# A graph and feed-forward layer on one core: score buffer moved behind x's parts, and one row tile rounded a step later

## What is computed

```python
xn = layernorm(x)
support = xn @ W                                      # graph layer
g = segment_sum(support[src] * edge_weight[:, None], dst)   # 42500 edges
q = xn @ Wq.T + bq; k = xn @ Wk.T + bk; v = xn @ Wv.T + bv  # 16 heads of 64
q /= norm(q); k /= norm(k)                            # norms of the whole matrices
s = (phi(q) * phi(k)).sum(-1)                         # phi: exp of a map per head
x = x + g + s * v / s
r = act_quant(layernorm(x))                           # rows rounded to 8 bits
x = x + act_quant(silu(r @ Wg.T) * (r @ Wu.T)) @ Wd.T # Wg, Wu, Wd ternary
```

## Time and profile before

| | us |
|---|---|
| median of 3 runs | 1653.69 (1653.36 to 1654.15) |
| the profiled execution, whole | 1655.15 |
| its span, first to last instruction | 1653.4 |
| PE busy in it | 1623.9 |
| DVE busy | 1132.4 |
| ACT busy | 497.1 |
| POOL busy | 713.9 |

### The profile page before, as it was taken

The page is one execution under the profiler, slowest core; times in us unless marked ns, Lnnn a source line. Parts: engine busy times, 40 slices in busy tenths (PEclk is TensorE's granted clock), DMA queues, the critical chain, the costliest instruction groups (busy, mean ns, idle before and its releaser), DMA issues.

```text
span 1653.4 us, 21995 instructions
## 1 busy us (share of the span) xinstructions
PE 1623.9 (98%) x7680; PEld 1336.2 (81%) x7680; DVE 1132.4 (68%) x2622; ACT 497.1 (30%) x640; POOL 713.9 (43%) x577
## 2 busy tenths in 40 slices
PE   7999999899999999999999999999999999999998
PEld 6899999688878888887888888888888888887665
DVE  7887793476787776656555566677757667576796
ACT  4644311222121111114211113333423324233554
POOL 2011555677777777777678605533130120300200
PEclk9999999899999999999999999999999999999999
DMA  9999888765686756557866656577383563742954
GB/s 315 352 410 354 294 269 261 204 139 126 134 210 149 198 131 151 148 142 168 230 148 130 137 154 196 162 189 197 101 195 116 124 161 99 158 127 76 240 157 125
DMA packets 164010, 304.94 MB, mean 184 GB/s; under 512 B 62856, under 2 KB 103624, under 8 KB 163945
## 3 DMA queue, kind: packets, MB, share of 16 engines
q1 hardware_dynamic: 77853, 204.77, 38.9%
q0 software_dynamic: 80272, 82.55, 24.3%
q10 hardware_dynamic: 5820, 16.88, 2.9%
HBM read 202.88 MB, written 101.24 MB: 184 GB/s over the span
## 4 chain that ended last, share of the span: by engine, by line
PE 76%; DMA 12%; DVE 5%; issue 4%; POOL 2%; SPq 1%; ACT 0%; DVEq 0%; POOLq 0%; ACTq 0%
PE PS L402 24%; PE PS L404 24%; PE PS L403 24%; DMA A_dense<-zeros 5%; DMA A_dense<-wtot,cell 5%; POOL A_dense L747 2%; PE PS L1886 2%; PE PS L1916 1%; DVE fin L1572 1%; DMA X<-in_x 1%; DVE stats L1157 1%; DMA rt<-z 1%; DVE hid L1546 0%; DVE ring L1176 0%; DVE h_sc L1549 0%
## 5 line engine op out<-in xcount | busy, mean ns | idle before, releaser
L747 POOL DMA_INDIRECT A_dense<-wtot,cell x333 | 537.6, 1615 | 217.4 <-DMA A_dense<-wtot,cell 123.0
L402 PE MATMUL PS<-AL,SH 125*128 125x500 f32 x784 | 306.3, 391 | 0.0
L404 PE MATMUL PS<-AH,SH 125*128 125x500 f32 x784 | 305.1, 389 | 0.0
L403 PE MATMUL PS<-AH,SL 125*128 125x500 f32 x784 | 304.6, 389 | 0.0
L402 PE MATMUL PS<-WL,xtH 128*125 128x512 f32 x640 | 252.5, 394 | 0.7 <-DVE xtL L1296 0.7
L403 PE MATMUL PS<-WH,xtL 128*125 128x512 f32 x640 | 252.1, 394 | 0.0
L404 PE MATMUL PS<-WH,xtH 128*125 128x512 f32 x640 | 251.9, 394 | 0.0
L1033 ACT ACTIVATE SH<-S 125x1024 fp32r<-125x1024 f32 x98 | 104.0, 1061 | 333.0 <-PE PS L404 333.0
L1410 DVE TENSOR_TENSOR SL<-S,SH 125x1024 fp32r<-125x1024 f32 x98 | 119.6, 1220 | 120.3 <-ACT SH L1033 120.1
L404 PEld LDWEIGHTS PS<-AH,SH 125*128 125x128 f32 x784 | 147.8, 189 | 31.4
L403 PEld LDWEIGHTS PS<-AH,SL 125*128 125x128 f32 x784 | 147.1, 188 | 31.0
(11 more groups left out here) (202 smaller groups left out, 2660.2 us busy)
## 6 DMA issues: line engine op xcount, KB each, us to landing
A_dense<-zeros POOLq DMA_DIRECT2D x40, 1280.0 KB, 9.1
xt<-xnT SPq DMA_DIRECT2D x60, 500.0 KB, 6.2
Araw<-A_dense SPq DMA_DIRECT2D x100, 250.0 KB, 2.7
Aside<-A_dense SPq DMA_DIRECT2D x100, 250.0 KB, 3.0
keyrow<-key_rows SPq DMA_DIRECT2D x42, 512.0 KB, 4.2
ewrow<-weight_rows SPq DMA_DIRECT2D x42, 512.0 KB, 5.5
xnT<-XT ACTq DMA_DIRECT2D x20, 500.0 KB, 8.2
zx<-in_x SPq DMA_DIRECT2D x20, 448.0 KB
```

The costliest lines, as they stand in the source:

```text
L402: nc.tensor.matmul(o, lh, rl, start=start, stop=False)
L403: nc.tensor.matmul(o, ll, rh, start=False, stop=False)
L404: return nc.tensor.matmul(o, lh, rh, start=False, stop=stop)
L747: pool.indirect_dma_start(cells[m], bass.IndirectOffsetOnAxis(cell[:, col:col + 1], 0), wtot[:, col:col + 1], None, compute_op=ALU.add).th ...
```

## The change

The parts of x now start at 196800: `xt` (to 204800), `xtH` and `xtL` of slot 0 (to 212800) and of slot 1 (to 220800). `ex` and `zx` follow (220800 to 228992), so that now the second half of `ex`, the one of odd tiles, lies over `zeros`. `bdk` moves to the last 4096 bytes of `Gs` (214720 to 218816), under the two parts of slot 1. DVE's wait for the strips goes from before the first write of `xtL` of slot 1 to before the first write of the second half of `ex`, at t == 1 and behind its wait for tile 1's products. In the feed-forward part the fourth tile of the last group is rounded at step 14 and not 13; `largest_r` goes from the end of step 12 to the end of step 13, `round_r` and `scales_back` to the end of step 14.

```diff
@@ -78,7 +78,7 @@
-ROUNDED_AT = (8, 10, 12, 13)
+ROUNDED_AT = (8, 10, 12, 14)
@@ -211,16 +211,16 @@
-    bdqk = (bdq, zone("E1f", at, END_AT)("bdk", [P, KT, P]))
     late = E_AT + 20 * D
     assert at <= late
-    ex = zone("E1x", late, END_AT)("ex", [P, 2, D])
-
-    zx = zone("E2x", late, END_AT)("zx", [P, 2, D])
-    e2 = zone("E2", cursor["E2x"], END_AT)
+
+    e2 = zone("E2", late, END_AT)
     xt = e2("xt", [P, 2, KT, ROWS])
     xtH, xtL = zip(*[[e2(f"xt{x}{i}", [P, KT, ROWS], F32R) for x in "HL"] for i in range(2)])
-    e2s = zone("E2s", cursor["E2x"], cursor["E2x"] + 4 * 4 * KT * ROWS)
+    bdqk = (bdq, zone("E1f", at + 4 * (NB * 512 - KT * P), END_AT)("bdk", [P, KT, P]))
+    zx = zone("E2x", cursor["E2"], END_AT)("zx", [P, 2, D])
+    ex = zone("E1x", cursor["E2"], END_AT)("ex", [P, 2, D])
+    e2s = zone("E2s", late, late + 4 * 4 * KT * ROWS)
@@ -1310,14 +1310,14 @@
             i = t % 2
-            if t == 0:
-                for c in range(2):
-                    dve.wait_ge(s_Azero[c], 16 * A_PITCH // P)
             low_of_tile(1 - i, t // 2 + i)
...
             dve.wait_ge(s_mm[i], t // 2 + 1)
+            if t == 1:
+                for c in range(2):
+                    dve.wait_ge(s_Azero[c], 16 * A_PITCH // P)
             if t >= 2:
                 dve.wait_ge(s_red[i], t // 2)
@@ -1597,12 +1597,14 @@
-        dve.wait_ge(s_f6, TILES * 4 - 1)
-        scales_back(slice(TILES - GT, TILES))
-        dve.wait_ge(s_fb, 2)
         for t in range(TILES - GT - 2, TILES - 2):
             hidden(t // 2, t % 2)
             add_down(t - 1)
+            if t == ROUNDED_AT[-1]:
+                round_r(GROUPS - 1, GT - 1)
+                dve.wait_ge(s_f6, TILES * 4 - 1)
+                scales_back(slice(TILES - GT, TILES))
+                dve.wait_ge(s_fb, 2)
```

## The result

The changed kernel took 1642.85 us (median of 4 runs, 1640.8 to 1643.7) against 1653.77 us (4 runs, 1653.36 to 1654.15) before. The ratio is 0.9932, 95% interval 0.9915 to 0.9949: 0.7% faster, 10.9 us by the medians. The forecast was 1641.5 in a range of 1639.5 to 1645. By the median alone rival 1 (only part one pays, 1643.4) lies nearer; what decides between the two is the traces. The profiled execution took 1640.8 us, with a span of 1639.0.

The account below looks back on a forecast made before the run. PE was taken as the bound, busy 1623.9 of 1653.4 us. Removing the gap and slow restart (10.3 us) and feed-forward stalls (1.9) gave 12.2 us off 1653.69, so 1641.5 us, range 1639.5 to 1645.

Parts of the forecast that it names:

- rival 1: Feed-forward part gains nothing because another input of `hidden(13)` or `(14)` is late; 1643.4 us, chance 11%.
- part one: Map loop: moving DVE's wait for strips removes PE's gap and slow restart between tiles 0 and 1, 10.3 us.
- The gap and the slow restart: Between map tiles 0 and 1 on PE: 7.50 us of gap plus 2.84 us of half-pace matmuls, together 10.3 us.
- Rival 2: Slow restart returns elsewhere, or something else in the shifted stages stops PE 2 to 8 us; 1644 to 1650, 5%.
- What is late next: Moved wait before tile 1's bias sum finds strips landed by 316.3, with 4.9 us in hand until 321.2.
- the second margin: Up to tile 3's split, wanted at 332.3 and done 6.5 us after the bias sum begins: strips at 325.8 cost nothing.
- The addresses at no cost: Address moves issue nothing and existing waits keep the order of `bdk` and slot 1; costed at zero.
- The gain lasts: POOL's indirect DMAs end at 943.5, landing about 947; SP loads the matrix at 954.9, leaving 8 us.
- rival 5: POOL's chain of indirect DMAs becomes the bound through shared-port holds; time could reach about 1721 us, chance 3%.
- The fourth tile: Feed-forward steps 13 to 15: later rounding removes PE's stalls at steps 13 and 14, 0.19 us left; gain 1.87 us.
- a second part at 0: Upper end of the forecast's own range: the feed-forward rounding change gains nothing, giving 1643.4 us.
- a small new wait: Allowance of 1.6 us above in the forecast range, for a wait the change might newly bring.

Follow-up runs that it names:

- filling the gap alone: Kernel before with 31 matmuls of unused result between map tiles 0 and 1: 1652.25 us against 1653.79, ratio 0.9994.
- the kernel with the tail part alone: Kernel before with only the fourth tile's rounding moved to step 14, old layout and old wait: 1651.24 us against 1652.86, ratio 0.9988.
- the kernel with the map part alone: Changed kernel with the fourth tile's rounding back at step 13, leaving the new layout and moved wait: 1644.48 us, ratio to before 0.9955.
- The delay experiments: 16 matmuls (3.7 us) added ahead of map tile 0: kernel before 1654.27 us against 1653.79; changed kernel 1646.02 us, 3.1 us above its 1642.9.
- the first set: The first set of experiments; the kernel before ran beside it at 1643 to 1657 us.
- the kernel with early strips: Kernel before with the second part's strips issued earlier, two ahead of each of the first three pairs, then one: 1644.93 us against 1654.85, ratio 0.994.

## Why the prediction was right, point by point

**The gap and the slow restart: 10.3 us forecast, 10.36 measured** between the start of map tile 0 and step 0. Both terms stand by themselves: the moved wait closes the gap, and filling the gap alone gives back 2.7 us up to step 0 and 3.0 in all (2.84 forecast). The terms are those of one execution, though. In the traces of the kernel with the tail part alone and of the one with the new layout and the old wait, the gap cost 7.0 and 7.4 us and the slow restart 2.2 and 2.1, together 9.2 and 9.5. Rival 2, a return of the slow restart elsewhere, did not come: the granted clock is 1.00 through the stretch.

**What is late next.** DVE's bias sum waited for PE and not for a strip, as forecast. The margin in front of it was mis-sized: 4.9 us, less 2.2 to 2.6 for the added traffic, was forecast, and 0.8 us was left in the first trace of the changed kernel and 2.8 in the second. The landing of the last strip took 12.8 and 14.5 us in them, and 14.0 in the kernel with the map part alone, against 10.6 before and 10.1 and 10.5 in the two others with the old wait, so the traffic cost 2.2 to 3.9 us. In the first trace PE had also reached the map loop 1.9 us earlier, and the last strip was issued 0.4 us later. It cost nothing, since DVE may be late there: the second margin, up to the split of tile 3, was the one that mattered. Its working (the split done 6.5 us after the bias sum begins, so strips at 325.8 are just free) had the right instruction and a size 0.4 us too small. It was read from tile 0, and behind tile 1's bias sum the edge work is longer (6.9 us). Strips at 325.77 cost PE 1.3 us, in a trace whose map loop had begun 1.1 us earlier than the one of the forecast.

**The addresses at no cost:** right as far as the runs can tell, by the kernel with the new layout and the old wait (ratio 1.0008, 0.9989 to 1.0027).

**The gain lasts:** right. SP's first load of the edge matrix came at 952.93, POOL's last indirect DMA ended at 937.25 + 1.55 = 938.8. The slack from there was 14.1 us, where the forecast's numbers give 11.4 (8 with a landing), since POOL's chain also ended 4.7 us earlier. POOL's 333 instructions averaged 1617 ns (1615 before), so rival 5, holds of the shared port, had no effect that the trace shows. Long ones are not as rare as the prediction says: from 300 to 400 us, 12 of 43 took over 1.7 us before and 7 of 44 after. That they are port holds is not shown. The Trainium skill's rule on that port ("SBUF — State Buffer", section "Who interferes with whom") was neither confirmed nor contradicted by this.

**The fourth tile: 1.87 us forecast, 1.82 measured.** The three starts of `hidden` were forecast at 1605.50, 1611.48 and 1617.76. Step 12 comes 12.58 us earlier in the changed kernel's trace, which puts them at 1592.92, 1598.90 and 1605.18. DVE's timeline:

```profile
1592.92 0.74 DVE L1546 SCALAR_TENSOR_TENSOR hid<-PS,u_back,gate 125x512 f32<-125x512 f32 x1
...
1598.90 0.74 DVE L1546 SCALAR_TENSOR_TENSOR hid<-PS,u_back,gate 125x512 f32<-125x512 f32 x1
...
1605.18 0.75 DVE L1546 SCALAR_TENSOR_TENSOR hid<-PS,u_back,gate 125x512 f32<-125x512 f32 x1
```

All three agree to 0.01 us, and the remaining stall at step 15 was 0.23 us for a forecast of 0.19.

**The step that was off: from the profiled execution to the median.** The forecast took 12.2 us from 1655.15 and then 1.46 more, because the profiled execution of before lay that far above its median. The first figure, 1643.0, is close to the measured 1642.85, but that is in part luck: it was a forecast of the profiled execution, and this took 1640.8, since its map loop began 1.9 us early. The measured median is 1.35 us above the forecast, on the side where the range had no room for the offset (it put 1.4 us for it below). It stayed inside because the upper end allowed for a second part at 0 and a small new wait, and neither came.

The delay experiments show why such an offset need not carry over. Before, the time from the start to map tile 1 was set by POOL's strips, and what PE lost or won ahead of that was swallowed. After, it is set by PE's own list. The two kernels vary for different reasons, and an offset of the one says nothing about the other. The two other traces with the old wait say where most of it lay: gap and slow restart cost 10.3 us in the profiled execution and 9.2 and 9.5 in those, and 1653.69 less some 9.4 and 1.8 is 1642.5. So the 12.2 us of a somewhat costly execution were taken off the median of cheaper ones. That this holds for the four runs behind the median is likely but not shown, as only one run of that kernel has a trace.

The same explains the spread of the kernel before on another chip. Of its 24 runs beside the first set, five took 1643.5 to 1645.6 us and the rest 1650.3 to 1656.9. The five lie where the kernel with early strips lies (1643.9 to 1645.7). Their mean granted clock over the run is 0.998 or 0.999, as in most runs of the kernels without a gap (0.997 to 0.999), and that of the others 0.994 to 0.998. That in those five the strips landed before DVE asked for them is a reading from the times, with no trace of such a run.

Not explained: 0.32 us between steps 6 and 7, where the distance of the turnings was 6.61 us before, 6.29 after, 6.32 in the second trace of the changed kernel, and 6.11 in the kernel with the tail part alone. It is PE's wait for `hq` at the turning of step 7, 0.59 us before, 0.28 and 0.30 after, and none there; it varies among kernels that do not differ in this place.

## What to carry to other kernels

A buffer's place can cost as much as an instruction: if the first work that PE waits for lies over memory that a slow chain is still using, give that place to a buffer that is written later, or start the chain earlier. Price such a wait as the gap plus the slow steps behind it, then ask which instruction queued behind the new place of the wait PE needs first. When the wait that goes had been hiding variation of the work ahead of it, take the sum off the profiled execution itself, and expect the runs of the new kernel to vary for other reasons than those of the old one. They need not spread more: the first four runs spread 0.8 us before and 2.9 after, but in the later sets the kernel before spread over 4.6 to 13.4 us and the changed kernel's six runs over 2.6.

## What the runs showed of the hardware

After a rest of 7.33 us, 14 steps of matmuls of 512 columns took 6.09 us, most of them 0.43 us each, and then each took 0.23. That is 2.84 us lost, and it is the largest loss of the six traces with such a rest. The loss does not grow with the rest:

| rest, us | steps over 0.25 us | lost against 0.232 us a step, us |
|---|---|---|
| 3.35 | 10 | 1.64 |
| 6.82 | 11 | 2.25 |
| 7.22 | 11 | 2.12 |
| 7.33 | 14 | 2.84 |
| 7.73 | 10 | 2.00 |
| 13.25 | 9 | 1.74 |

The stall of 1.45 us in the feed-forward part left no slower steps behind it: the granted clock stayed 1.00, and the next turning came after 5.85 us and its own stall of 0.26 and a remainder of 0.17, the one after that in 5.87 us.

A further strip (1280 KB) at the end of the chain took 3.0 us with DVE and its loads at rest, and 3.2 to 4.3 us beside the map loop's loads (from the last regular issue to the landing of two more 21.3 us and of four more 27.7, against 12.8 and 14.5 without them). The last strip's landing went from 10.1 to 10.6 us in three traces to 12.8, 14.0 and 14.5 us when the loads that DVE's wait had held back ran beside it.
